# Head roots spread by DMA, and second attention's probabilities split in two half-precision parts and turned by DMA transposes

## The reference

```python
h = tok(x)                    # rfft2 of 16x16 patches, real part, weights, projection, + position
h = h + attn(layernorm(h))    # 12 heads of 16, softmax over the queries' axis (axis=2)
h = h + ffn(layernorm(h))     # the second attention:
    gates, mask = softmax(x @ wg), top-2 of 10 routed heads (+ 2 shared heads)
    q, k, v = x @ qkv_w + qkv_b           # 12 heads of 64
    q, k = layernorm(q) * w + b, layernorm(k) * w + b      # over each head's 64
    o = softmax(q @ k.T / 8) @ v
    o = masked_gates[..., None] * o       # one factor per token and head
    return o @ proj_w + proj_b
```

## Time and profile before

| | |
|---|---|
| median of three runs | 5536.64 us |
| profiled execution's span | 5532.4 us |
| one image in the steady part of the span | 42.01 us |
| busy in 42.00 us of it: PE, DVE, ACT, POOL | 41.44, 38.07, 33.75, 23.26 us |
| DMA | 19 GB/s mean, 106 MB |

### The profile page before, as it was taken

The page is one execution under the profiler, slowest core; times in us unless marked ns, Lnnn a source line. Parts: engine busy times, 40 slices in busy tenths (PEclk is TensorE's granted clock), DMA queues, the critical chain, the costliest instruction groups (busy, mean ns, idle before and its releaser), DMA issues.

```text
span 5532.4 us, 202492 instructions
## 1 busy us (share of the span) xinstructions
PE 5344.4 (97%) x63024; PEld 4563.7 (82%) x63024; DVE 4923.8 (89%) x16193; ACT 4327.1 (78%) x17409; POOL 2985.7 (54%) x3206
## 2 busy tenths in 40 slices
PE   3999999999999999999999999999999999999998
PEld 2788888888888888888888888888888888888887
DVE  5899999999999999999999999999999999999996
ACT  1777887887888788788778878877887887887786
POOL 0555555555555555555555555555555555555554
PEclk9999999999999999999999999999999999999999
DMA  2000000000000000000000000000000000000000
GB/s 72 18 22 18 17 21 17 18 17 21 18 17 21 17 18 17 21 18 17 21 18 17 20 18 18 17 21 18 17 21 17 18 17 21 18 17 21 18 17 6
DMA packets 60519, 106.93 MB, mean 19 GB/s; under 512 B 8076, under 2 KB 33944, under 8 KB 60128
## 3 DMA queue, kind: packets, MB, share of 16 engines
q1 hardware_dynamic: 60456, 106.12, 6.2%
HBM read 86.72 MB, written 19.37 MB: 19 GB/s over the span
## 4 chain that ended last, share of the span: by engine, by line
PE 94%; DVE 4%; issue 1%; ACT 0%; POOL 0%; SPq 0%; DVEq 0%; DMA 0%; POOLq 0%; ACTq 0%
PE bank L491 82%; PE bank L672 10%; PE bank L529 2%; DVE qk L898 1%; DVE qkn L996 1%; SPq L403 0%; ACT p L733 0%; DMA bp<-in_bp 0%; ACT pq L771 0%; POOL pq L475 0%; DVEq L902 0%; DVEq L1025 0%; DVE wqk_mean L804 0%; DVEq L992 0%; DVE nmax L903 0%
## 5 line engine op out<-in xcount | busy, mean ns | idle before, releaser
L475 POOL TENSOR_TENSOR pq<-pq,gn 99x788 f32<-99x788 f32 x768 | 1153.3, 1502 | 914.0 <-DVE gn L1011 913.9
L771 ACT ACTIVATE pq<-bank,nmax 99x197 f32<-99x197 f32 x3072 | 1300.1, 453 | 291.6 <-DVE nmax L1002 291.6
L733 ACT ACTIVATE p<-bank,nmax 99x197 f32<-99x197 f32 x3072 | 1323.1, 467 | 112.0 <-DVE nmax L903 97.3
L484 POOL TENSOR_TENSOR qkb<-qkn,ln_b 128x396 f32<-128x396 f32 x768 | 639.5, 847 | 1164.0 <-DVE qkn L996 1151.4
L777 ACT ACTIVATE pT<-bank 99x394 f32<-99x394 f32 x1536 | 767.6, 518 | 259.4 <-PE bank L672 256.4
L903 DVE TENSOR_REDUCE nmax<-bank 99x2 f32<-99x394 f32 x1536 | 843.2, 563 | 113.9 <-PE bank L491 101.7
L1002 DVE TENSOR_REDUCE nmax<-bank 99x2 f32<-99x394 f32 x1536 | 827.2, 559 | 25.7 <-PE bank L491 10.7
L733 ACT ACTIVATION_READ_ACCUMULATOR p<-bank,nmax 99x1 f32 x3072 | 762.6, 248 | 0.0
L491 PE MATMUL bank<-x2T,wqkc 128*128 128x198 f16 (+1 forms) x7680 | 752.5, 248 | 1.0 <-ACT p L733 0.7
L672 PE MATMUL bank<-ident,pq 99*99 99x99 f32 (+1 forms) x6144 | 725.3, 253 | 7.7 <-ACT pq L771 5.2
L771 ACT ACTIVATION_READ_ACCUMULATOR pq<-bank,nmax 99x1 f32 x3072 | 720.7, 235 | 0.0
(11 more groups left out here) (148 smaller groups left out, 10116.0 us busy)
## 6 DMA issues: line engine op xcount, KB each, us to landing
xa<-in_xa SPq DMA_DIRECT2D x128, 300.1 KB
xb<-in_xb SPq DMA_DIRECT2D x128, 300.1 KB
out_tokens<-res SPq DMA_DIRECT2D x128, 74.2 KB
out_tokens<-res SPq DMA_DIRECT2D x128, 73.5 KB
p<-in_wq SPq DMA_DIRECT2D x1, 1152.0 KB
pT<-in_wk SPq DMA_DIRECT2D x1, 1152.0 KB
...
```

What stands on the lines that cost most here:

```text
L475: nc.gpsimd.tensor_tensor(pair, pair, factor, op=ALU.mult).then_inc(s_sc.up(), 1)
L484: nc.gpsimd.tensor_tensor(qkb[:, t], qkn[:, t % QKN_SLOTS], ln_b[:].unsqueeze(2).to_broadcast([128, 2, TP]), op=ALU.add).then_inc(s_qk.up( ...
L733: last = nc.scalar.activation(p1[0:TC, h, c, :], psum("s1", h)[0:TC, c * T:c * T + T], ACT.Exp, bias=nmax1[:, c, h:h + 1], accum_out=sum1[ ...
L771: last = nc.scalar.activation(pq[0:TC, h % SLOTS, c, 0:T], psum("s2", h)[0:TC, c * T:c * T + T], ACT.Exp, bias=nmax2[:, h, c:c + 1], accum ...
```

## The change

Roots: instead of a selecting matmul per pair of heads, DVE writes one full-precision tile `rs`; SP stores it to DRAM and reads it back six times, each row repeated over 64 partitions, into `rsb`; POOL multiplies q and k by it (`mul`), and ACT scales and shifts (`aff`), in place of DVE's L996 and POOL's `bias`. Probabilities: after `sc`, DVE rounds a pair's 792 columns to half precision (`hi`), POOL subtracts that to get the low part (`lo`), and SP turns both parts with two DMA transposes of 112 rows x 1024 columns (`tr`); the identity matmuls and ACT's copies go. The values are split by ACT (high) and DVE (low), and `o2` is three half-precision products (high x high, high x low, low x high). Beside these, the gate's logits ride in 14 more columns of two of the four `v2` products, the variance of a token comes from BN_AGGR, and the images are up to four ahead (three before). All lists are new, and SP has one.

```diff
-            def bias(img, t):
-                pool.wait_ge(*read_out(img, "rstd", t))
-                nc.gpsimd.tensor_tensor(qkb[:, t], qkn[:, t % QKN_SLOTS], ln_b[:]..., op=ALU.add).then_inc(s_qk.up(), 1)
+            def low(img, t):
+                pool.wait_ge(*s_ph.at(img, t + 1))
+                nc.gpsimd.tensor_tensor(probs_part(t, 1), probs(t), probs_part(t, 0), op=ALU.subtract).then_inc(s_pl.up(), 1)
+            def times_rstd(img, t):
+                pool.wait_ge(*s_rsb[t // 2].at(img, 32))
...
+                nc.gpsimd.tensor_tensor(qkn[:, t % QKN_SLOTS], qkc[:, t], rsb[:, t], op=ALU.mult).then_inc(s_qn.up(), 1)
+            def root_out(img, _):
+                sp.wait_ge(*s_rs.at(img, 1))
+                sp.dma_start(root_rows, rs[:]).then_inc(s_rsw.up(16), 16)
+            def root_in(img, _):
+                by_head = root_rows.rearrange("(u c j) n -> j c u n", u=4, c=16, j=2)
+                sp.wait_ge(*s_rsw.at(img, 16))
+                for n in range(3):
+                    for j in range(2):
+                        sp.dma_start(rsb[64 * j:64 * j + 64, 2 * n:2 * n + 2]...,
+                                     by_head[j, n].unsqueeze(0).to_broadcast([64, 4, TP])).then_inc(s_rsb[n].up(16), 16)
+            def turn(img, t):
+                sp.wait_ge(*s_pl.at(img, t + 1))
+                for c in range(2):
+                    sp.dma_start_transpose(pT[:, t, :, c, :], pqh[:, t % PAIR_SLOTS, c]...).then_inc(s_tr[t].up(16), 16)
...
-                pe.wait_ge(*read_out(img, "pT", 2 * t + 1))
-                        last = mm(o[64 * j:64 * j + 64, 0:T], v2[:, c, E2 * h:E2 * h + E2], pT[:, h, c, :], c == 0, c == 1)
+                pe.wait_ge(*s_tr[t].at(img, 32))
+                    for n, (v, p) in enumerate(((0, 0), (0, 1), (1, 0))):
+                            last = mm(o[64 * j:64 * j + 64, 0:TP]..., v2[0:TC, v, c, E2 * h:E2 * h + E2],
+                                      pT[0:TC, t, 4 * j + 2 * p + c, :, 0:TC], c + n == 0, c + n == 3)
...
+            def affine(img, t):
+                act.wait_ge(*s_qn.at(img, t + 1))
+                for s in range(2):
+                    last = nc.scalar.activation(qkb[:, t, s, :], qkn[:, t % QKN_SLOTS, s, :], ACT.Identity, bias=ln_b[:, s:s + 1], scale=ln_w[:, s:s + 1])
...
-                step(V.scalar_tensor_tensor(rootsq[:], lnvar[:], -3.0, root[:], ALU.add, ALU.mult), img, "var", 1)
-                step(V.tensor_scalar(rs_mask[:], rootsq[:], low_rows[:, 0:1], None, ALU.mult), img, "var", 2)
-                V.scalar_tensor_tensor(rs_hl[:], rootsq[:], -0.5, rs_mask[:], ALU.mult, ALU.subtract).then_inc(s_rs.up(), 1)
+                V.scalar_tensor_tensor(rs[:], lnvar[:], -3.0, root[:], ALU.add, ALU.mult).then_inc(s_rs.up(), 1)
...
+            def high(img, t):
+                dve.wait_ge(*s_sc.at(img, t + 1))
+                V.tensor_copy(probs_part(t, 0), probs(t)).then_inc(s_ph.up(), 1)
```

The lists of DVE, POOL and SP after the change:

```diff
+    "dve": 0:hi3 0:gr4 0:s2_11 3:qk1_0 0:gr5 3:s1_0 1:var2 0:hi4 3:s1_1 3:qk1_1 3:s1_2 0:hi5 3:s1_3 0:ol0 2:cl1 0:ol1 3:qk1_2
+ 3:s1_4 2:cl2 3:s1_5 3:s1_6 3:s1_7 4:fold 2:wo 0:ol2 0:ol3 1:v2_0 1:s2_0 1:s2_1 2:nx2 0:ol4 1:s2_2 1:s2_3 3:ctx0 1:v2_1
+ 1:v2_2 1:v2_3 2:x2T 1:s2_4 1:gl 0:ol5 1:gate1 1:gate2 1:gate3 1:gr0 3:cl0 1:s2_5 3:ctx1 1:gr1 4:tok 1:hi0 1:gr2 3:s1_8
+ 1:hi1 1:s2_6 3:s1_9 3:s1_10 4:nx1 1:s2_7 1:hi2 3:s1_11 0:proj 1:gr3 4:x1T 1:s2_8 1:s2_9 1:s2_10 3:ctx2
+    "pool": 1:mul4 1:mul5 3:h1b 2:sq0 2:sq1 1:sc0 1:sc1 2:sq2 1:lo0 4:root1 1:sc2 2:sq3 1:lo1 1:lo2 1:sc3 2:sq4 2:sq5 1:lo3 1:sc4
+ 1:sc5 1:lo4 1:lo5 1:h2c 2:h2b 2:mul0 2:mul1 2:mul2 2:mul3 3:root2
+    "sp": 0:tr3 1:rsw0 1:rsb0 4:load 0:tr4 0:tr5 1:tr0 0:store 1:tr1 1:tr2
```

More of the change, by code:

```diff
@@ L131 @@
     "pe": """
[L132 to L136, removed]
+0:o2_3@5 1:v2_0@6 1:s2_0@42 0:o2_4@7 1:s2_2@50 0:o2_5@3 1:v2_1@1 1:v2_2@2 1:v2_3@7 2:x2T@4 1:s2_4@65 3:ctx0@1 2:qk0@7
@@ L137 @@
+2:qk1@2 4:tok@3 2:qk2@7 2:qk3@4 3:s1_8@10 3:s1_10@27 1:s2_6@45 2:qk4@6 0:proj@1 4:x1T@3 2:qk5@2 1:s2_8@65 1:s2_10@01
+4:qk1_0@3 2:ms0@7 2:ms1 4:v1@6 1:o2_0@2 2:ms2 4:s1_0@34 4:qk1_1@0 3:ctx1@1 4:s1_2@37 4:qk1_2@5 1:o2_1@0 3:ctx2@6
+4:s1_4@24 1:o2_2@3 4:s1_6@07 3:wo@1
 """,
     "dve": """
-3:fold 1:var2 0:gr5 0:ol1 2:wo 1:rstd0 1:rstd1 3:tok 0:ol2 0:ol3 0:ol4 3:nx1 0:ol5 1:s2_0 1:s2_1 1:gate3 1:s2_2 1:s2_3
-1:v2_0 3:x1T 2:nx2 1:rstd2 3:qk1_0 0:proj 3:s1_0 3:s1_1 3:s1_2 1:s2_4 3:qk1_1 3:s1_3 1:v2_1 1:gr0 1:v2_2 1:s2_5 1:v2_3
@@ L141 @@
-1:gr1 2:x2T 3:s1_4 3:qk1_2 1:rstd3 3:s1_5 3:ctx0 3:s1_6 1:gr2 1:s2_6 1:s2_7 1:rstd4 3:s1_7 1:rstd5 2:gl 3:s1_8 3:ctx1
-1:gr3 3:s1_9 2:gate1 3:s1_10 1:s2_8 3:s1_11 1:s2_9 2:gate2 3:ctx2 1:s2_10 1:gr4 3:cl0 3:cl1 3:cl2 1:ol0 1:s2_11
+0:hi3 0:gr4 0:s2_11 3:qk1_0 0:gr5 3:s1_0 1:var2 0:hi4 3:s1_1 3:qk1_1 3:s1_2 0:hi5 3:s1_3 0:ol0 2:cl1 0:ol1 3:qk1_2
+3:s1_4 2:cl2 3:s1_5 3:s1_6 3:s1_7 4:fold 2:wo 0:ol2 0:ol3 1:v2_0 1:s2_0 1:s2_1 2:nx2 0:ol4 1:s2_2 1:s2_3 3:ctx0 1:v2_1
+1:v2_2 1:v2_3 2:x2T 1:s2_4 1:gl 0:ol5 1:gate1 1:gate2 1:gate3 1:gr0 3:cl0 1:s2_5 3:ctx1 1:gr1 4:tok 1:hi0 1:gr2 3:s1_8
@@ L143 @@
+1:hi1 1:s2_6 3:s1_9 3:s1_10 4:nx1 1:s2_7 1:hi2 3:s1_11 0:proj 1:gr3 4:x1T 1:s2_8 1:s2_9 1:s2_10 3:ctx2
 """,
     "act": """
[L145 to L148, removed]
+1:v2_0 1:aff1 1:aff2 1:s2_0 1:s2_1 0:o2_4 0:o2_5 1:v2_1 1:s2_2 1:v2_2 1:v2_3 2:x2T 1:s2_3 1:gate0 2:qk0 3:ctx0 2:qk1
@@ L149 @@
+1:s2_4 1:s2_5 1:aff3 2:qk2 2:qk3 3:s1_8 1:aff4 3:s1_9 2:qk4 3:s1_10 1:s2_6 1:s2_7 1:aff5 4:x1T 2:qk5 3:s1_11 1:s2_8
+1:s2_9 1:s2_10 4:qk1_0 1:s2_11 2:var0 2:var1 4:v1 4:s1_0 4:qk1_1 1:o2_0 3:ctx1 4:s1_1 4:s1_2 1:o2_1 4:qk1_2 3:ctx2
+4:s1_3 1:o2_2 4:s1_4 4:s1_5 4:s1_6 4:s1_7 2:aff0 1:o2_3
 """,
     "pool": """
-3:root1 1:bias2 3:h1b 1:h2c 2:h2b 1:sc0 1:sc1 1:bias3 2:sq0 1:sc2 2:sq1 1:bias4 1:bias5 2:sq2 2:sq3 2:sq4 1:sc3 2:sq5
-1:sc4 1:sc5 3:root2 2:bias0 2:bias1
+1:mul4 1:mul5 3:h1b 2:sq0 2:sq1 1:sc0 1:sc1 2:sq2 1:lo0 4:root1 1:sc2 2:sq3 1:lo1 1:lo2 1:sc3 2:sq4 2:sq5 1:lo3 1:sc4
@@ L181, in bank_uses, with build_vit_block @@
     return uses, in_bank
-def build_vit_block(nc, ins, out, images):
+def build_vit_block(nc, ins, out, root_rows, images):
     with ExitStack() as ctx:
@@ L854, in moments @@
                 step(last, img, name, 1)
[L856 to L862 removed]
+                V.memset(vare[n][:], LN_EPS)
+                for c in range(2):
+                    last = V.bn_aggr(both[n][:, c, :], stats[n][:, c, :])
+                step(last, img, name, 2)
+                V.tensor_tensor(vare[n][:], both[n][:, :, 1], vare[n][:], op=ALU.add).then_inc(s_mv[layer].up(), 1)
             def normalise(img, layer, src, dst, sig, name):
@@ L867, in normalise @@
                 for c in range(2):
-                    last = V.tensor_scalar(dst[:, c, :], src[:, c, :], mean[layer][:, c:c + 1], rstd[layer][:, c:c + 1],
+                    last = V.tensor_scalar(dst[:, c, :], src[:, c, :], both[layer][:, c, 0:1], rstd[layer][:, c:c + 1],
                                            ALU.subtract, ALU.mult)
```

219 lines of the change are left out of this document (109 added, 110 removed).

## The result

The changed kernel takes 7036.22 us (median of four, 7031.2 to 7042.01), the kernel before beside it 5536.76: 1.271 times as long, 95% interval 1.269 to 1.273. The forecast was 5957 us with a range of 5100 to 6450; the time lies above it.

The account below looks back on a forecast made before the run. PE set the pace before; after the change DVE would, with 35.7 us of work plus 9.4 of waits beside POOL, 45.1 an image. 128 x 45.1 = 5773, plus 180 fill and drain and 4.2, gave 5957 us (5100 to 6450).

Parts of the forecast that it names:

- DVE's own work: DVE per image: removed and added instructions take its need from 38.1 to 35.7 us, waits not counted.
- waits beside POOL: DVE instructions reading two SBUF tiles, or rounding from SBUF, wait for POOL's instruction in flight: 9.4 us an image.
- The 0.07 us of its own start: On DVE, some 14 waits each hide about 0.07 us of an instruction's start, taking 10.4 us to 9.4.
- covers a trip to DRAM and back: From rs to mul0: POOL does 5 us of work and DVE reaches s2_0 some 10 us later, covering the roots' trip.
- The third rival: DMA queue: SP works in order; a transpose holding it above 3.2 us passes 45.1; at 3.6, 6580 us; chance 0.07.
- PE waiting for `tr`: Sign on PE: waiting for the transposes would prove the forecast wrong in the way of the DMA queue rival.
- price T: Time one transpose holds SP's queue: an image needs 12 T + 6.7 us; nothing in the trace prices it.
- 128 x 45.1: Sum over images: DVE's 45.1 us an image taken as the period for 128 images, 5773 us.
- fill and drain: Pipeline ends: 155 us as before plus 25 for one more image of depth with two DMA trips, 180 us.
- waits of 7 to 13 us: The main forecast's span of DVE waits per image, with its own range 5640 to 6400 us and chance 0.58.
- half the waits: Rival on DVE: only 3 to 6 us of waits, DVE needing 39 to 42, say 40.1 us: 5317 us; chance 0.20.
- no waits: Rival: the lock does not bite, a loop of POOL and DVE takes 37.4 us an image: 4971 us; chance 0.13.

Follow-up runs that it names:

- e12: e7 with POOL's scaling also left out but for two columns of 197 per head (computation incomplete): 5571.67 us, 0.6% over the kernel before.
- e2: Changed kernel with the low parts of the probabilities left out but for one column of 99 (computation incomplete): 6721.44 us.
- e8: Changed kernel with the load early, the store behind the transposes and the six squares moved from POOL to ACT: 6156.99 us, 1.113 of the kernel before.
- e1: Changed kernel with the load of the pixels issued right after the sixth transposes in SP's list, ahead of the wait for the roots' trip: 6575.86 us.
- e4: e1 with the third and fifth gn put ahead of the rounding before them in DVE's list: 6575.74 us.
- e7: e3 with the roots' trip through DRAM left out, queries and keys multiplied by ones (computation incomplete): 5727.02 us.
- e11: e1 with the roots' trip through DRAM left out, multiplied by ones instead, low parts in full (computation incomplete): 6389.75 us.
- e3: Changed kernel with both the early load and the low parts left out but for one column of 99 (computation incomplete): 6301.71 us.

## Why the prediction was wrong

**Right: DVE's own work and its waits beside POOL.** 35.7 + 9.4 = 45.1 us an image, 5773 us in all, against 5800.2 busy; e12 leaves 35.7 for the work alone. e2 and e8 show that the waits are POOL's doing. That the sum fits to 0.5% is in part luck: with the load early (e1) `fold` is held too, as the forecast had it, and DVE is busy 5981 us. Of the places, `gn` fits (3.4 us over its bare length in six, 3.2 forecast for four of them); others do not (`hi` 1.7 against 0.8, `gfac` 0.6 against nothing), and in e4 the places moved while the time stayed. A `gn` beside a `lo`, as in the earlier trace rows:

```profile
3543.95 1.64 POOL L511 TENSOR_TENSOR pqh<-pq,pqh 99x792 f16<-99x792 f32 x1 [0.64 <-DVE pqh L1041]
```

```profile
3543.99 1.61 DVE L1033 TENSOR_TENSOR gn<-rsum,mg 99x4 f32<-99x4 f32 x1
```

The 0.07 us of its own start that each wait was to hide stands in no row; this `gn` ends 0.01 us after the `lo`, so it hid about 0.15 of its 0.17.

**The step that failed: DMA.** It weighed the bytes (4.8 MB forecast, 4.9 measured) and asked whether the roots are back before `mul0`: "covers a trip to DRAM and back". It never asked what SP holds behind the wait for that trip. The first thing is the load of the pixels, for the `fold` of the same pass: 735 us. The third rival looked at this queue, but through the wrong number: a transpose holds it 1.4 us, far under the 3.2 from which that rival would decide (six in a row, in e1):

```profile
3501.17 8.38 SPq L456 DMA_TRANSPOSE pT<-pqh  x6
```

It was order, not occupation: the load waits for the trip, and its bytes for those of the copies. The sign that the prediction named for this rival, PE waiting for `tr`, did come (3.9 us an image), without the price T that it stood for: some transposes stand behind the trip and the load too, and without the trip's entries in SP's list (e7) PE waits 0.1 us an image for them.

**Then the sum.** "128 x 45.1" takes DVE's work for the period, with only 180 us for fill and drain. DVE was idle for 499 us beside `fold`'s wait, and no run here went under 431. The miss is 27 us of busy time + 735 + 319 = 1081, of 1079. In the steady 1500 us above, DVE idles 85 us beside `fold`'s 154, some 3 us an image, for results of ACT and PE and in short gaps; the forecast put this at nothing. This step alone is enough to fail: with the load early (e1) the time is still 619 us over the forecast and above its range, by 208 us more of busy time and 404 more of idle time in the profiled run.

**The trip covered?** In the changed kernel nearly: `mul` waits 0.7 us an image for `rsb`, and in e11 the trip is worth 1.2.

```profile
L524 POOL TENSOR_TENSOR qkn<-qkc,rsb 128x396 f32<-128x396 f32 x768 | 769.4, 1025 | 114.9 <-DMA rsb<-root_rows 90.9 <-ACT qkb L787 20.5
```

Not where DVE is quicker: 4.0 us of waits in e3, and 4.4 us an image between e3 and e7.

**Sizes.** PE 42.5 us, not 34.3: twelve products take 0.70 us (4.2 for 72, not 3.1) and more at the lower clock; in e12, at a clock of 0.99, PE needs 37.9, and some 2.5 us of that over 34.3 stay unexplained. That PE was busy 77% of the span, near the 76% forecast, is luck: more work in a longer span. DVE was to be busy over 95% and was at 82. ACT's `aff` takes 569 ns, not 370; `mul` 1025, not 850; `lo` 1641, not 1500. The rounding's median is 566 ns, near the 0.5 taken, so its strides are not dear. None of these engines was busy for as long as DVE. Two readings of the working were slightly off and change nothing: the earlier trace rows holds eight of the ten gate products, and waits of 7 to 13 us give 5650 to 6420 us, not 5640 to 6400. Of the rivals, "half the waits" and "no waits" are refuted by DVE's busy time and by `gn` at 733 ns.
